# A graph layer in two-term products: layer-norm batches one step later, pieces of two blocks up to step 23, first transfers sorted over two queues

## The reference

```python
h = jnp.maximum(_layernorm(x, axis=-1), 0.0)      # eps 1e-5
support = jnp.matmul(h, W)
out = x + relu(jnp.matmul(adj, support) + b)
```

## Time and profile before

| | |
|---|---|
| median of 3 runs | 725.02 us (724.86 to 725.10) |
| the profiled execution's own time | 724.92 us |
| its span, first to last instruction | 723.1 us |
| TensorE busy | 715.5 us (99%) |
| VectorE busy | 619.0 us (86%) |
| ScalarE busy | 513.7 us (71%) |
| GpSimd busy | 167.6 us (23%) |
| moved by DMA | 281.60 MB, mean 389 GB/s |
| granted TensorE clock | full in all 40 slices of the span |

### The profile page before, as it was taken

One profiled execution on the slowest core, in us unless ns is written; L12 is line 12 of the kernel. 1 busy time (PEld: TensorE's weight loads), 2 busy tenths in 40 slices (PEclk: granted clock), 3 DMA queues, 4 the chain that ended last, 5 costly groups with the idle time before them and its releaser, 6 DMA issues.

```text
span 723.1 us, 7868 instructions
## 1 busy us (share of the span) xinstructions
PE 715.5 (99%) x3125; PEld 586.1 (81%) x3125; DVE 619.0 (86%) x371; ACT 513.7 (71%) x378; POOL 167.6 (23%) x99
## 2 busy tenths in 40 slices
PE   8999999999999999999999999999999999999997
PEld 4878888888888888888888888888888888888886
DVE  5989999989999888988789888888888888888894
ACT  2888888888887767756667766667676767767562
POOL 3326555444455202321011000000000000133123
PEclk9999999999999999999999999999999999999999
DMA  9999999999999999999999999999999999999992
GB/s 354 405 416 415 416 417 415 416 415 415 416 415 412 386 393 406 406 372 400 376 403 398 416 411 392 375 377 398 392 382 380 396 379 394 388 411 394 376 377 74
DMA packets 42805, 281.60 MB, mean 389 GB/s; under 512 B 4880, under 2 KB 5520, under 8 KB 29200
## 3 DMA queue, kind: packets, MB, share of 16 engines
q1 hardware_dynamic: 41904, 278.94, 96.5%
q10 hardware_dynamic: 864, 2.16, 0.8%
HBM read 276.89 MB, written 4.19 MB: 389 GB/s over the span
## 4 chain that ended last, share of the span: by engine, by line
PE 93%; DMA 5%; DVE 1%; ACT 0%; SPq 0%; issue 0%; ACTq 0%; DVEq 0%
PE banks L560 92%; DMA raw<-adj 5%; PE banks L587 0%; PE banks L588 0%; PE banks L586 0%; DVE low L518 0%; ACT high L380 0%; PE banks L602 0%; SPq L244 0%; ACT L364 0%; DVE x_sb L481 0%; DVE x_sb L489 0%; ACTq L370 0%; DVEq L150 0%; ACTq L379 0%
## 5 line engine op out<-in xcount | busy, mean ns | idle before, releaser
L518 DVE TENSOR_TENSOR low<-raw,high 128x1536 fp32r<-128x1536 f32 (+2 forms) x239 | 573.9, 2420 | 88.1 <-PE banks L560 76.4
L380 ACT ACTIVATE high<-raw 128x1536 fp32r<-128x1536 f32 (+2 forms) x239 | 479.6, 2017 | 189.9 <-DMA raw<-adj 166.1
L560 PE MATMUL banks<-high,h_high 128*128 128x512 f32 x1012 | 269.0, 390 | 0.6 <-ACT high L380 0.6
L560 PE MATMUL banks<-high,h_low 128*128 128x512 f32 x1012 | 268.4, 389 | 0.0
L560 PE MATMUL banks<-low,h_high 128*128 128x512 f32 x1012 | 268.0, 390 | 0.2 <-DVE low L518 0.2
L560 PEld LDWEIGHTS banks<-high,h_high 128*128 128x128 f32 x1012 | 189.8, 188 | 41.3 <-ACT high L380 1.2
L560 PEld LDWEIGHTS banks<-low,h_high 128*128 128x128 f32 x1012 | 189.6, 188 | 40.6 <-DVE low L518 1.4
L560 PEld LDWEIGHTS banks<-high,h_low 128*128 128x128 f32 x1012 | 189.9, 188 | 39.5
L331 POOL TENSOR_SCALAR x_sb<-x_sb,bias 128x512 f32<-128x512 f32 x16 | 52.7, 3297 | 420.1 <-DMA x_sb<-x_blocks 420.1
L322 POOL TENSOR_SCALAR z_sb<-x_sb,neg_mean,rstd 128x128 f32<-128x128 f32 x60 | 79.8, 1342 | 1.6
L307 POOL TENSOR_TENSOR rstd<-var_eps,minus_half 128x4 f32<-128x4 f32 (+2 forms) x17 | 34.5, 2028 | 122.7 <-DVE var_eps L423 112.4
(11 more groups left out here) (34 smaller groups left out, 49.9 us busy)
## 6 DMA issues: line engine op xcount, KB each, us to landing
raw<-adj SPq DMA_DIRECT2D x106, 1536.0 KB, 8.9
raw<-adj SPq DMA_DIRECT2D x113, 768.0 KB, 10.1
raw<-adj SPq DMA_DIRECT2D x20, 512.0 KB, 12.0
x_sb<-x_blocks SPq DMA_DIRECT2D x16, 256.0 KB, 8.4
out_blocks<-x_sb SPq DMA_DIRECT2D x15, 256.0 KB, 8.9
x_sb<-x SPq DMA_DIRECT2D x14, 256.0 KB, 11.6
raw<-adj SPq DMA_DIRECT2D x3, 256.0 KB, 6.6
raw<-adj ACTq DMA_DIRECT2D x1, 768.0 KB, 11.3
```

What stands on the lines that cost most here:

```text
L380: nc.scalar.activation(high[:, t % HIGH_SLOTS, cols], raw[:, t % RAW_SLOTS, cols], ACT.Copy).then_inc(high_ready, 1)
L518: nc.vector.tensor_tensor(low[:, t % LOW_SLOTS, cols], raw[:, t % RAW_SLOTS, cols], high[:, t % HIGH_SLOTS, cols].bitcast(F32), ALU.subtra ...
L560: return nc.tensor.matmul(banks[:, FIRST_BANK[g] + c, :], h[:, (t - FIRST_STEP[g]) * DEPTHS[g] + k, :], tile[:, slot, at:at + BANK], start ...
```

## The change

- `NARROW_UNTIL` goes from 8 to 24: steps 8 to 23 come in three pieces of two blocks.
- The x batches from 4 on move one step later: load and mean in phase 1 (steps 5, 9, ...), squares in phases 2 and 3, variance in phase 3.
- The rectifying moves from phase 2 to phase 3, one step ahead of use; batch 2 stays in step 2. Its place is after the step's last piece while there are three, and after the first of two from step 24 on (for batch 2: after the last piece instead of between pieces 1 and 2).
- Of the first transfers, ScalarE's queue keeps piece 1 of step 0 and x batches 1 and 2; piece 3 of step 0 and piece 1 of step 1 go to SP's queue, in the order of need.
- W and b are loaded after step 30's pieces, and halved in steps 36 and 38.

```diff
-NARROW_UNTIL = 8
+NARROW_UNTIL = 24
 def mean_at(t):
-    return batch_at(t, 0, 3)
+    return batch_at(t, 1, 3) if t >= 5 else None
 def variance_at(t):
-    return batch_at(t, 2, 3) if t >= 4 else None
+    return batch_at(t, 3, 3) if t >= 7 else None
 def rectified_at(t):
-    return batch_at(t, 2, 2)
+    return 2 if t == 2 else batch_at(t, 3, 2) if t >= 7 else None
 def squares_at(t):
-    j = batch_at(t, t % 4, 3) if t >= 4 and t % 4 in (1, 2) else None
+    j = batch_at(t, t % 4, 3) if t >= 6 and t % 4 in (2, 3) else None
...
-    at = BATCHES[j][0] + (t % 4 - 1) * 2
+    at = BATCHES[j][0] + (t % 4 - 2) * 2
@@ sync
-            for t in range(FOUR_PASS):
-                for i in range(0, len(split_of(t)), 2):
-                    load_piece(t, i)
-            for t in range(FOUR_PASS, ALL_STEPS):
+            for i in (0, 2, 3):
+                load_piece(0, i)
+            for t in range(1, ALL_STEPS):
...
-                if t == 7:
+                if t == 30:
                     sp.dma_start(W_sb[:, :], W).then_inc(params_landed, 16)
@@ scalar
-            for j, (t, i) in ((1, (0, 1)), (2, (0, 3)), (None, (1, 1))):
-                act.dma_start(raw[:, t, columns_of(t, i)], adj_piece(t, i)).then_inc(raw_landed[t][i], 16)
-                if j is not None:
-                    first, end = BATCHES[j]
-                    at = first % 4 * P
-                    act.dma_start(x_sb[:, x_slot(j), at:at + (end - first) * P], x_batches[j]) \
-                       .then_inc(x_landed[x_slot(j)], 16)
+            act.dma_start(raw[:, 0, columns_of(0, 1)], adj_piece(0, 1)).then_inc(raw_landed[0][1], 16)
+            for j in (1, 2):
+                first, end = BATCHES[j]
+                at = first % 4 * P
+                act.dma_start(x_sb[:, x_slot(j), at:at + (end - first) * P], x_batches[j]) \
+                   .then_inc(x_landed[x_slot(j)], 16)
...
-                    if i == len(split_of(t)) - 2 and rectified_at(t) is not None:
+                    if i == (0 if t >= NARROW_UNTIL else len(split_of(t)) - 1) and rectified_at(t) is not None:
                         rectify(rectified_at(t))
...
-                if t == 9:
+                if t == 36:
                     act.wait_ge(params_landed, 32)
@@ vector (the same edit for rectified_low, and)
-                if t == 13:
+                if t == 38:
                     dve.wait_ge(W_high_ready, 1)
```

## The result

The changed kernel takes 722.46 us (median of 6 runs, 722.28 to 722.60), the kernel before 725.18 us in the same comparison (6 runs, 724.86 to 726.04). The ratio is 0.9961, with a 95% interval of 0.9950 to 0.9973: faster by 2.7 us. The profiled execution took 722.60 us with a span of 720.8 us, against 724.92 and 723.1: 2.3 us less.

The account below looks back on a forecast made before the run. TensorE's products bound the kernel, with 1.86 us lost between steps 3 and 12, where loads are bandwidth-bound. Step 12 moving from 59.67 to 57.95 gains 1.72 us: from the median 725.02 to 723.3, range 722.2 to 725.2.

Parts of the forecast that it names:

- rival A: The forecast by itself, with a time of 722.9 to 723.9 us; chance 55%.
- The loads hold step 8, and the bytes ahead of it count: Step 8's first copy waits for bandwidth-bound loads; fewer bytes ahead let step 8 start 0.96 us earlier, at 41.48.
- 0.16 us for the bytes of W and b: Ahead of step 8: moving the loads of W and b (64.5 KB) to step 30 saves 0.16 us by bytes.
- Can TensorE be there by 41.48? Yes, even with no gain at the start: TensorE before step 8: step 6 at 33.33 gives step 8 at 41.49, without the start's gain.
- rival B: One DMA engine's delay, put down to an instruction transfer, strikes where nobody waits: landings 1.3 us earlier, 722.0 us; chance 14%.
- The filled hole is worth nothing at the end: TensorE's 1.48 us wait ahead of step 2: 1.3 us filled, then given back at steps 6 to 8.
- 0.15 us in steps 8 to 11: Loss booked for VectorE's extra work in step 9, against TensorE's need; bounds 0 and 0.9 us.
- Step 12 at 57.95: Forecast start of step 12 on TensorE, against 59.67 before: 1.72 us gained.
- What follows step 12 keeps its length: Everything from step 12 to the end takes as long as before, so the forecast is step 12's start.
- C: Another microsecond is lost, by a second delay or VectorE's crowd in steps 9 and 10: 724.3 us; chance 20%.
- D: Step 8's start is not decided by the bytes but by something that stays: 725.0 us; chance 4%.
- E: VectorE becomes the bound in steps 8 to 23, past a subtraction pitch of 1.235 us: 726.9 us; chance 7%.

Follow-up runs that it names:

- e12: Changed kernel with W and b loaded after step 7's pieces and halved in steps 9 and 13, as before the change: 722.72 us.
- e6: Changed kernel plus 112 tiny VectorE instructions in steps 90 to 96, written to a tile nobody reads: 723.41 us.
- e7: Changed kernel with the early block (halves of tiles 0 and 1, on VectorE) made in step 40 instead of step 9: 722.12 us.
- e10: Changed kernel with 4 warming products instead of 8 ahead of step 0: 722.59 us.
- e2: Changed kernel with the first transfers issued as before the change, on both queues: 722.28 us.
- e1: Kernel before with only the first transfers sorted as in the change: 726.16 us.
- e11: Changed kernel with x batches loaded behind their step's pieces, halves of tiles 0 and 1 made in step 40, and 4 warming products: 722.98 us.
- e4: Kernel before with only the later x batches, rectifying, W and b moved as in the change; wide pieces and first transfers kept: 725.12 us.

## Why the prediction was right, and where it was wrong

The forecast was 723.3 with 722.2 to 725.2, faster; measured 722.46 and 2.7 us faster. It is inside the range, below the 722.9 to 723.9 that rival A, the forecast by itself, allowed. The mechanism of the first 60 us held; of the two numbers that make the time, the gain there was put too high and the gain behind the last product was missing. That the two errors partly cancel is luck.

- *The loads hold step 8, and the bytes ahead of it count*: held. The first copy of step 8 was forecast for 40.42 behind ScalarE's own work, and began at 40.41. Step 7's last and step 8's first piece were forecast to land at 38.18 and 39.46 and came at 38.13 and 39.42. The 0.16 us for the bytes of W and b did not show in that: with them back ahead of step 8 (e12) its first piece lands 0.03 us later (the first of its shares 0.31), in one execution of each.
- *"Can TensorE be there by 41.48? Yes, even with no gain at the start"*: this step failed, by 0.31 us. It took step 6 at 33.33 at the latest; it was 33.57. The prediction knew the delayed share and, in rival B, that its cause would recur, but left its place out of this check. In the changed kernel it fell on step 5's last piece (30.46 instead of 29.03), and so it did in e6, e7 and e12, which are the same up to there (30.24 to 30.33). e10 and e2, where it strikes a later piece, have no hole there.
- *The filled hole is worth nothing at the end*: held, and more: e1 keeps 0.15 of 1.06 us, e2 is no slower without it.
- *0.15 us in steps 8 to 11*: 0.31 measured, of it 0.29 in step 10. e7, without the early block, loses nothing there; the block was one of the two extras that the prediction named.
- *Step 12 at 57.95*: 58.42 in the changed kernel, so 1.25 us instead of 1.72. e2 had 57.99.
- *"What follows step 12 keeps its length"*: this step failed. It holds for the products, to 0.01 us, and not for the last store: 1.09 us came from the place of an instruction transfer. Both errors together, -0.47 and +1.09, are the 0.6 us between 723.2 and the profiled 722.6; the median of the kernel before rose by 0.16 as more runs came in. e6, which has the old tail, took 723.41, near the forecast of 723.3.
- *Rival B* named a nearer time than the forecast (722.0) by a mechanism that did not occur: the late share was there. *C* and *D* did not occur. *E* did not either (from step 12 on TensorE is on pace), but its point was closer than reckoned. VectorE's timeline, the answer to the earlier trace rows:

```profile
50.21 6.89 DVE L516 TENSOR_TENSOR low<-raw,high 128x1024 fp32r<-128x1024 f32 x6
57.03 0.68 DVE L463 SCALAR_TENSOR_TENSOR h_low<-z_sb,h_high 128x512 fp32r<-128x512 f32 x1
...
57.70 7.19 DVE L516 TENSOR_TENSOR low<-raw,high 128x1024 fp32r<-128x1024 f32 x6
```

Six in a row make a pitch of (7.19 - 1.24)/5 = 1.19 us beside GpSimd and 1.13 without it, against a limit of 1.235. The prediction had reckoned with 1.13 alone.

## What to carry to other kernels

Where loads are bound by bandwidth and barely outrun the engine, find the step at which the engine last waits and count what is issued ahead of it; time won before that step is given back there, and what is lost before it may cost nothing (the hole in e2, the slow start in e10). Smaller pieces help by raising how late a step's data may come, and only if the engines between have no extra work in front of the same step. Smaller pieces also change an engine's count of instructions. A difference of a microsecond may come from where an engine's instruction count stands at the end; compare the stretch behind the last product before giving it to a cause.

## What the runs showed of the hardware that was not expected

- A 16 KB instruction transfer on q8 at 28.28 us made one of sixteen shares of a landing 1.5 us late (30.46, the other fifteen by 28.96); an 8 KB one on q14 made the last store 1.1 us longer. TensorE did not stall for its own instructions: in the kernel before nine such 16 KB transfers pass, some 29 us apart, under its unbroken run of 1098 products. The Trainium skill (Runtime: NRT & Kernel Launch, Instruction fetch mechanics) calls such a fetch mostly hidden. That is so here for TensorE, which fetches, not for the DMA that stands behind it.
- The moment alone doesn't say which piece is struck: with transfers at 28.01 to 28.28 us (changed kernel, e6, e7, e12) it was step 5's last piece, due at some 29.0, and with transfers at 28.15 (e2) and 28.42 (e1) it was the one after it. The order of the issues differs in these two; which part of it decides stays open.
- With 4 warming products instead of 8, TensorE was idle ahead of step 0 for 2.12 us in e10 (waiting for the first h) and for 1.70 in e11 (for a piece of adj). The records of L600 then began 0.85 us apart or more, up to 8.82 us in e10 and up to 10.06 in e11; the later ones, from 10.79 on in e11, and nearly all of the changed kernel are 0.43 apart. L600 of e10, then of e11:

```profile
5.24 12.35 PE L600 MATMUL banks<-raw,h_first 128*128 128x512 f32 x24 [2.12 <-DVE h_first L448]
```

```profile
4.81 13.44 PE L600 MATMUL banks<-raw,h_first 128*128 128x512 f32 x24 [1.70 <-DMA raw<-adj]
```

The view gives the granted clock of the stretch from 4 to 8 us of e10 as 1.00, the level of 2.4 GHz. But the trace's own list of granted clocks begins only at 8.87 us in e10 and at 10.66 in e11 (at 4.50 in the changed kernel), which is where the pace changes, and the view counts a stretch that the list lacks as full. In e4, with eight warming products, the same is seen: two records 0.98 and 0.86 us apart, full pace from 7.09, a list that begins at 6.72. Twice the distance fits the level of 1.2 GHz; no row says so.
